# The two parts of dt added by GpSimd behind its last u of a step, in place of VectorE's sum in C's bank

## The reference

```python
xn = layernorm(x)
# branch 1: a state-space scan, N = 32 states for each of D = 256 channels
dt = softplus(xn @ dt_w.T + dt_b)
A = -exp(log_A)
b, c = xn @ B_w.T + B_b, xn @ C_w.T + C_b
h_t = exp(A * dt_t) * h_{t-1} + (dt_t * x_t) * b_t
y_t = sum_n(h_t * c_t) + D_skip * x_t
# branch 2: a mixture of 8 experts, the two best per row, 1024 -> 256 with relu
out = x + y + moe(xn)
```

## Time and profile before

| | |
|---|---|
| median of 3 runs | 3822.43 us (3817.44 to 3827.14) |
| the profiled execution | 3817.81 us |
| its span | 3816.1 us |
| VectorE busy | 3647.8 us, 96% |
| GpSimd busy | 3261.9 us, 85% |
| ScalarE busy | 2564.6 us, 67% |
| TensorE busy | 3229.2 us, 85% |

### The profile page before, as it was taken

The page is one execution under the profiler, slowest core; times in us unless marked ns, Lnnn a source line. Parts: engine busy times, 40 slices in busy tenths (PEclk is TensorE's granted clock), DMA queues, the critical chain, the costliest instruction groups (busy, mean ns, idle before and its releaser), DMA issues.

```text
span 3816.1 us, 64710 instructions
## 1 busy us (share of the span) xinstructions
PE 3229.2 (85%) x16548; PEld 2095.9 (55%) x16548; DVE 3647.8 (96%) x2281; ACT 2564.6 (67%) x4811; POOL 3261.9 (85%) x1722
## 2 busy tenths in 40 slices
PE   7776888888888888888888888888888888888887
PEld 4354555555555555555555555555555555555554
DVE  7787999999999999999999999999999999999998
ACT  3245677677776777767676767767676677767775
POOL 0017999999998999999998999999999999999996
PEclk9888999999999999999999999999999999999999
DMA  9975555555656556555656556465656555565555
GB/s 327 341 115 150 162 163 160 174 144 145 169 163 179 168 150 173 153 153 162 164 165 179 164 153 157 136 180 156 170 162 180 163 159 136 147 191 158 165 169 163
DMA packets 345305, 645.57 MB, mean 169 GB/s; under 512 B 49405, under 2 KB 221441, under 8 KB 344641
## 3 DMA queue, kind: packets, MB, share of 16 engines
q1 hardware_dynamic: 252018, 538.77, 43.8%
q0 software_dynamic: 67776, 85.24, 14.1%
q10 hardware_dynamic: 25104, 16.91, 2.0%
HBM read 515.55 MB, written 142.80 MB: 173 GB/s over the span
## 4 chain that ended last, share of the span: by engine, by line
issue 30%; DVE 25%; POOL 18%; PE 12%; ACT 7%; DMA 6%; DVEq 1%; POOLq 1%; SPq 1%; ACTq 0%
DVE hc L1214 12%; POOL u L1026 11%; DVE h L1225 10%; PE bank L639 3%; POOL out_rows L985 3%; PE bank L648 3%; ACT bank L798 2%; POOL xg L973 2%; DMA dt<-x 2%; DMA dt<-dt_rows 2%; PE bank L494 2%; ACT xgt L802 1%; POOL dtx_n L958 1%; ACT ht L840 1%; DMA bc_rows<-bcv 1%
## 5 line engine op out<-in xcount | busy, mean ns | idle before, releaser
L1026 POOL TENSOR_TENSOR u<-dtx,b_sb 128x1024 f32<-128x1024 f32 x1024 | 2514.5, 2523 | 146.1 <-DVE h L1225 102.7
L1225 DVE TENSOR_TENSOR_SCAN h<-bank,u 128x1024 f32<-128x1024 f32 x1024 | 2300.2, 2276 | 27.6 <-ACT bank L798 15.5
L798 ACT ACTIVATE bank<-dt,a_neg 128x1024 f32<-128x1024 f32 x1026 | 1129.0, 1108 | 401.7 <-DVE h L1225 309.7
L639 PE MATMUL bank<-xgt,w_sb 128*128 128x256 f32 x4096 | 1045.7, 400 | 257.3 <-ACT ht L840 216.6
L1214 DVE TENSOR_TENSOR hc<-h,bank 128x2048 f32<-128x2048 f32 x514 | 1163.6, 2264 | 44.9 <-ACT bank L868 44.3
L639 PEld LDWEIGHTS bank<-xgt,w_sb 128*128 128x128 f32 x4096 | 756.9, 195 | 636.7 <-issue 551.4
L648 PE MATMUL bank<-w_sb,ht 128*128 128x256 f32 x4096 | 936.4, 382 | 29.1 <-ACT o_sb L855 29.1
L648 PEld LDWEIGHTS bank<-w_sb,ht 128*128 128x128 f32 x4096 | 763.0, 191 | 221.4 <-issue 128.7
L840 ACT ACTIVATE ht<-bank,b_sb 128x256 f32<-128x256 f32 x1024 | 423.0, 463 | 288.4 <-PE bank L639 288.4
L598 PE MATMUL bank<-hc,rsum 128*32 128x512 f32 x4112 | 551.0, 608 | 2.5 <-DVE hc L1214 2.5
L985 POOL DMA_INDIRECT out_rows<-o_sb,sidx x258 | 415.4, 1610 | 55.6 <-issue 36.2
(11 more groups left out here) (114 smaller groups left out, 1821.9 us busy)
## 6 DMA issues: line engine op xcount, KB each, us to landing
b_sb<-bc_rows SPq DMA_DIRECT2D x258, 512.0 KB, 4.1
c_sb<-bc_rows SPq DMA_DIRECT2D x258, 512.0 KB, 4.2
dt<-dt_rows SPq DMA_DIRECT2D x132, 512.0 KB, 7.6
dtx<-dtx_rows SPq DMA_DIRECT2D x132, 512.0 KB, 5.2
w_sb<-w SPq DMA_DIRECT2D x18, 1024.0 KB, 7.7
dt_rows<-dt_n SPq DMA_DIRECT2D x137, 128.0 KB, 3.9
dtx_rows<-dtx_n SPq DMA_DIRECT2D x137, 128.0 KB, 1.8
out_rows<-y_sb POOLq DMA_DIRECT2D x34, 512.0 KB, 6.7
```

Source lines behind the costliest of these rows:

```text
L639: mm = pe.matmul(m_ps[:, c, :], w1_sb[:, kk, ch * P:(ch + 1) * P], xgt[:, kk, :], start=(kk == 0), stop=(kk == KD - 1))
L798: act.activation(a_ps[k % 2], dt[:, k % GPP, :], ACT.Exp, scale=a_neg[:, col:col + 1]).then_inc(a_ready, 1)
L1026: pool.tensor_tensor(u[:, k % UB, :], dtx[:, gp, :], b_sb[:, j, :], ALU.mult).then_inc(u_ready, 1)
L1225: dve.tensor_tensor_scan(h[:, k, :], a_ps[k % 2], u[:, k % UB, :], 0.0, ALU.mult, ALU.add).then_inc(scan_done, 1)
```

## The change

`prep_dt` is no longer called in the steps. GpSimd gets a new function, `dt_part`, which it calls behind its u of k = 7: it waits for the logarithm, for the store of the piece before and for its own last `dtx_part`, and adds the two parts into dt_n. GpSimd's operands stand in SBUF here, so ScalarE writes the logarithm into za and no longer into bank 6. max(z, 0) is taken by ScalarE when it evacuates z: it reads z twice for each half of the channels, once with Relu into zv and once with Abs into za, and the instruction that made za later is gone. The logarithm follows the exponential at once, at k = 4, and the copy of C for the next step moves ahead, from k = 7 to k = 6, waiting for the last product with C.

```diff
             def evac_z(p):
                 act.wait_ge(dt_done, p + 1)
                 for g in range(KD):
-                    ins = act.activation(zv[:, g, :], z_ps[:, g * Q:(g + 1) * Q], ACT.Identity, bias=dtb[:, g:g + 1])
+                    act.activation(zv[:, g, :], z_ps[:, g * Q:(g + 1) * Q], ACT.Relu, bias=dtb[:, g:g + 1])
+                    ins = act.activation(za[:, g, :], z_ps[:, g * Q:(g + 1) * Q], ACT.Abs, bias=dtb[:, g:g + 1])
                 return ins
...
             def softplus(p):
 
-                act.activation(za[:], zv[:], ACT.Abs).then_inc(za_done, 1)
-                act.wait_ge(za_done, p + 1)
                 act.activation(ze[:], za[:], ACT.Exp, scale=-1.0).then_inc(ze_done, 1)
 
             def log_part(p):
                 act.wait_ge(ze_done, p + 1)
-                act.activation(zl_ps, ze[:], ACT.Ln, bias=1.0).then_inc(l_done, 1)
+                act.activation(za[:], ze[:], ACT.Ln, bias=1.0).then_inc(l_done, 1)
...
                         if i == 0:
                             act.wait_ge(c_in[1], 16 * (st + 2))
-                            act.wait_ge(dt_done, p + 2)
+                            act.wait_ge(hc_done, 4 * st + 5)
...
                             softplus(p)
+                            log_part(p)
                             c_copy(3)
...
                         if k == 6:
                             down_out(0)
-                            act.wait_ge(hc_done, 4 * st + 5)
-                            log_part(p)
-                        if k == 7:
                             c_copy(0)
+                        if k == 7:
                             down_out(1)
...
+            def dt_part(p):
+
+                pool.wait_ge(l_done, p + 1)
+                pool.wait_ge(dt_st, 16 * p + 1)
+                pool.wait_ge(prep_done, p + 1)
+                settle(pool)
+                pool.tensor_tensor(dt_n[:], zv[:], za[:], ALU.add).then_inc(dt_done, 1)
...
+                        if k == 7:
+                            dt_part(NG + 2 + st)
                         if k in (4, 6):
                             scatter(st, (s + 1) % 2, k // 2 - 2, 2 * b + ng if adds else None)
...
-                dve.scalar_tensor_tensor(out=dt_n[:], in0=zv[:], scalar=0.0, in1=zl_ps,
-                                         op0=ALU.max, op1=ALU.add).then_inc(dt_done, 1)
+                dve.tensor_tensor(dt_n[:], zv[:], za[:], ALU.add).then_inc(dt_done, 1)
...
                     if k % 2 == 0:
                         weigh(st, k // 2)
-                prep_dt(NG + 2 + st)
```

More of the change, by code:

```diff
@@ L169, in ssm_moe @@
         bc_ps = bank[0:2 * N, 6, KD * Q:(KD + 1) * Q]
-        zl_ps = bank[:, 6, KD * Q:2 * KD * Q].rearrange("p (k t) -> p k t", k=KD)
         turn_ps = bank[:, 6, :].rearrange("p (k s) -> p k s", s=SL)
@@ L241, in ssm_moe @@
         v_done = sem("v_done")
-        za_done = sem("za_done")
         ze_done = sem("ze_done")
@@ L932, in _ @@
                             down_out(0)
-                            act.wait_ge(hc_done, 4 * st + 5)
-                            log_part(p)
+                            c_copy(0)
                         if k == 7:
-                            c_copy(0)
                             down_out(1)
```

## The result

The changed kernel takes 3970.02 us (median of 5 runs, 3964.25 to 3986.29), the kernel before 3822.99 (5 runs). The ratio is 1.0395, 95% interval [1.0379, 1.0412]: 147 us slower. The forecast was 3899, in a range of 3847 to 3951. The profiled execution, the slowest of the five, took 3986.29 us with a span of 3983.9, against 3816.1 before.

What follows compares the result with a forecast made beforehand. VectorE was taken as the bound, at 26.57 us a step. Terms -40 (sum), +4 (copy of C), +69, +4 (waits for u), +20 and +21 (starts) made +78: 3896 on the profile, 3899 us for the runs, range 3847 to 3951.

Steps and rivals of the forecast that it cites:

- The sign: Whole kernel: slower through late dt loads, chance 0.75; slower by any route 0.85.
- Rival 2: GpSimd becomes the bound in every step, its step 26.6 us, time 3951; chance 0.10.
- rivals 1 and 3: 1: loads in time or GpSimd not held, faster, 3786, chance 0.09; 3: gain and losses cancel, 3822, chance 0.06.
- The step that failed: Last step of a half: dt 1 and dt 2 loads, four us later, land at 2.6 and 4.2, holding ScalarE.
- the third u as the tightest: After GpSimd's sum: the next step's third u is ready at 4.1 and needed at 6.6, enough for VectorE.
- forecast at 6.15: Mid-sequence half starts: dt 1 lands near 5.1, evacuation at 6.15 instead of 1.5; 4.3 us lost each, 16 x 4.3 = +69.
- the forecast's own term: Eight sequence starts without a change of expert: 3.9 us lost where 1.44 was before, 8 x 2.5 = +20.
- a shift of 2.1 us: Behind the held decay: ScalarE's evacuation comes at 3.65, 2.1 us late, and everything to the copy of C moves equally.
- the copy's slack: Steps that are no half start: copy of C moves 0.52 us against slack about 0.5, costing 0.04, 96 x 0.04 = +4.
- all of it in half starts: Profile sign: VectorE's wait for the copy of C grows from 41.8 to over 100 us, all in half starts.
- the new experts' starts: Seven sequence starts with a new expert: the same shift on top, 3 us each, 7 x 3 = +21.
- the forecast's +78: Sum of all terms, whole kernel, added to the profiled execution's 3817.8 us to give 3896.

Runs made afterwards that it cites:

- The clean run of the wait: Changed kernel with GpSimd's sum moved behind its third u of the next step, but the wait for the logarithm kept behind the last u: 3972.06 us, 1.0402.
- the best version: Kernel before plus the change with sum in the next step, old two-instruction evacuation, dt 0, 1, 2 loaded ahead of dtx 2 and 3: 3802.88 us, 0.9947.
- the kernel with dt loaded first (SyncE's order): Changed kernel with SyncE's loads of dt 0, 1 and 2 ahead of dtx 2 and dtx 3 in the last step of a half: 3896.09 us, 1.0198.

## Why the prediction was wrong

**Right.** The sign, and the wait as its cause. VectorE's plain step is 26.24 to 26.29 us where 26.26 was forecast (ng = 2). GpSimd's sum costs 0.68 from start to start (1568.06 to 1568.74) against the 0.70 taken:

```profile
1568.06 1.30 POOL L968 TENSOR_TENSOR dt_n<-zv,za 128x256 f32<-128x256 f32 x1
1568.74 2.92 POOL L1030 TENSOR_TENSOR u<-dtx,b_sb 128x1024 f32<-128x1024 f32 x1
```

In the two later steps of a half the logarithm ends 19.8 us after the first scan, as computed; in half of them GpSimd starts the sum as it comes, in the rest 1 to 2 us after it. Where GpSimd stops, it starts 0.29 us behind the logarithm's end (0.35 taken). In the middle of a sequence the last u slips behind the y DMAs, and dt 1 landed at 4.4 on the step's scale of 1573.47, where 5.1 was forecast. The clean run of the wait (1.0402) and the sum in the next step (1.0018) show that the wait is the whole of it. Rival 2 (GpSimd's work as the bound) is refuted by the same pair, rivals 1 and 3 by the result.

GpSimd was in fact less late than forecast: its last u ends 4.9 us before the next first scan in the middle of a sequence and 7.0 to 7.5 at a sequence's start (medians; 10.3 before), where the forecast had 3.6 and 6.1. So the loss is larger although the slip is smaller, and what was wrong is what the slip was taken to hold up.

**The step that failed** is "in the last step of a half the loads of dt tiles 1 and 2 for the next half stand behind that wait", taken as all that is late. Everything in SyncE's queue is: the dtx loads wait for u's, the store of dtx_n for GpSimd's product, and dt 0 stands behind them. Ahead of the half starts at 1302.43 and 1516.84 it was issued 13.6 and 12.2 us before the first scan in the kernel before, and 8.05 ahead of the one shown here (medians of the starts in the middle: 13.6 and 8.2). The front's list of SyncE's order has dt 0 behind dtx 2, and I gave it no term. Nor has the sum a term for GpSimd's idle time at a sequence's start: it takes the third u as the tightest, and there it is the first. What the two cost:

- The last step of a half takes +0.62 where the forecast had -0.1, 31 x 0.7 = 22 us. Ahead of the 16 starts in the middle of a sequence it is the first decay, late through dt 0 (4.19 us idle at 1572.15): VectorE waits 13.1 us there. Ahead of the 15 sequence starts it is the first u, late through GpSimd's slip and the idle time behind it: 15.2 us. With all loads of dt early this second wait stays, and grows to 34 us.
- In the middle of a sequence TensorE idles 3.74 us for the bank that ScalarE returns late, and its clock falls: 5.38 us for 16 products, not 3.69. The evacuation was forecast at 6.15 from dt 1 alone; it came at 6.46, waiting for TensorE although dt 1 was there earlier than I had it. The start is 0.86 over the forecast, 16 x 0.86 = 14 us. That the number is so near is luck: the forecast has the whole 4 us from dt 1, and with dt 1 first and dt 0 still issued at -8.5 the start keeps 3.2 us of its loss, which go when dt 0 is early too (dt 1 and dt 2 moved by 2.1 and 2.5 us as well between these two).
- At a sequence's start with the same expert it is the forecast's own term that is too small: dt 1 lands at 1.8 (median) where I had taken 2.6 and a shift of 2.1 us, and the loss is 4.75 and not 2.2, 8 x 2.55 = 20 us over. Moving dt 1 and dt 2 alone gives back 3.5 us of it and moving dt 0 alone 1.7, so both hold ScalarE there; how the two divide is not shown.

**A sign that came out otherwise.** I forecast that GpSimd would wait for the logarithm in nearly every step. It stops for more than 0.1 us in 47 steps, 160.6 us in all: in 31 half starts and in 16 steps behind one. In the half starts the logarithm itself is late, at 24.8 to 28.1 us (medians) and not at 19.8, since ScalarE has been standing for dt. So the delay feeds itself: late loads hold ScalarE, ScalarE's logarithm holds GpSimd, and GpSimd's u's hold the next loads. With the loads of dt early the stops are 15 and 22.9 us in all.

**A second miss** is the step behind a start. I took the copy's slack as 0.5 us in every step that is no half start ("so I take 0.04 us there"). That holds for ng = 2. In the step behind a start TensorE hands over its last products late (ScalarE waited 2.04 us for them at 1607.92, and 1.05 in the kernel before), so the slack there was gone already: VectorE waits 31.2 us for C in these steps, and 31 x 0.9 = 28 us go over the forecast. The run with two more evacuations shows 0.6 us a step of it on the kernel before; with the evacuation as before and the sum in the next step 26.8 us remain, so VectorE's 0.31 us is not won there either. So the sign "all of it in half starts" for the copy of C failed too: 31 of its 116.8 us stand here.

These come to 22 + 14 + 20 + 28 = 84 us, less 3 at the new experts' starts where I had taken more than was lost: +159 with the forecast's +78, where the profiled execution is at +168. Of the other 9 us, 2 lie ahead of the first scan and 3 behind the last step's start. On the medians the change is +147; this one profiled run was the slowest of five. Two slips of arithmetic in the forecast change nothing: 3896 and 4.6 make 3900 and not 3899, and 2 us in each of 31 half starts are 62 and not the 52 that give 3847.

**What stays open.** How the share of the clock and that of ScalarE's two stops divide in a half start was not separated on the chip; the trace alone shows the slow products. What holds GpSimd at a sequence's start is not shown: the profile calls that idle time "issue". Nor is it shown why the sequence starts are longer with the sum in the next step and the evacuation as before (29.5 and 33.2 us for same and new expert, 28.7 and 32.4 before; 30.9 and 32.3 in the best version), where a good part of VectorE's 40 us is lost again.

## What to carry to other kernels

An instruction moved to an engine that has time to spare is cheap only if it does not wait there: with the 0.7 us of work in another place the change was even (1.0018), the wait ahead of it cost 147 us, since it took the run-ahead by which GpSimd released buffers and hid its own idle time at each sequence start. When an engine that runs ahead is held, follow what it releases through the DMA queue, every entry of it in order, and not only the ones that stand right behind; here reordering that queue gave back 109 of 147 us. Look also for a way back from the last engine held to the first: a delay that returns there grows. And give the work a place where its input has long been made (here three blocks later): the same sum there, with the old evacuation and dt loaded first, runs at 0.9947 [0.9928, 0.9966] of the kernel before.

## What the runs showed of the hardware

- A sum of 128 x 256 on VectorE with one input in PSUM took 0.39 to 0.42 us beside GpSimd's products; with both inputs in SBUF it took 0.39 to 5.57 us (5.62 in another kernel) and ended with GpSimd's run of back-to-back products (430.51 to 435.75, while u ran from 430.82 to 435.46). The mean was 1428 ns over 138 and the kernel 2.4% slower for this operand alone. That is a price which the logarithm's place in C's bank had avoided. The Trainium skill, SBUF — State Buffer, "SBUF: two separate sides", says that VectorE with two SBUF inputs and a GpSimd instruction lock each other out for a whole instruction; here the lock outlasted two instructions of GpSimd.
- TensorE's clock: an idle time of 3.74 us was followed by a stretch with a granted clock of 0.57, in which 16 products took 5.38 us. With 0.28 us of idle time ahead of them they took 3.69. In the kernel with dt loaded first (SyncE's order), TensorE's timeline at the same half start has less idle time ahead of them, 2.34 us, and the same slow products, with a granted clock of 0.57 again:

```profile
1543.54 5.38 PE L645 MATMUL bank<-w_sb,ht 128*128 128x256 f32 x16 [2.34 <-ACT o_sb L851]
```
